# Local transformers on one core: transposes of 64 rows into two banks at a time, scores and transposes on two shared pairs of banks

## What is computed

```python
def _L0_ffn_ref(x, Wqkv, q_scale, k_scale, Wo, ln_g, ln_b, W1, b1, W2, b2):
    DIM, DEPTH, HEADS, DIM_HEAD, WINDOW, QK_SCALE = 128, 6, 16, 64, 32, 8.0
    def attn_layer(x, Wqkv, qs, ksc, Wo):
        q, k, v = split(x @ Wqkv)                    # 3 x 1024 channels, 16 heads of 64
        q = l2norm(q) * qs; k = l2norm(k) * ksc
        q = q * cos * scale + rotate_half(q) * sin * scale
        k = k * cos / scale + rotate_half(k) * sin / scale
        # a window of 32 queries sees the 32 keys of its window and the 32 before it
        sim = einsum('bhwie,bhwje->bhwij', q, k2) * QK_SCALE
        attn = softmax(where(mask, -max, sim), -1)
        return einsum('bhwij,bhwje->bhwie', attn, v2).reshape(...) @ Wo
    def ffn_layer(x, g, bln, W1, b1, W2, b2):
        xn = layernorm(x) * g + bln
        a, gate = split(xn @ W1 + b1)
        return a * gelu(gate) @ W2 + b2
    for i in range(DEPTH):
        x = attn_layer(shift_tokens(x), Wqkv[i], ...) + x
        x = ffn_layer(shift_tokens(x), ln_g[i], ...) + x
    return x
```

## Times and profile before

| what | value |
|---|---|
| runs (3) | 4911.07, 4916.79, 4919.24 us; median 4916.79 us |
| profiled execution | 4911.92 us, of which its span on the core 4909.9 us |
| first local transformer, first to last `down` (L1097) | 694.3 to 2389.1 us |
| second local transformer, first to last `down` | 2786.9 to 4480.5 us |
| one period in the steady state | 36.75 us |
| busy in that period | PE 35.10, PEld 25.04, DVE 32.91, ACT 32.21, POOL 24.49 us |
| granted TensorE clock there | 1.00 of 2.4 GHz |

### The profile page before, as it was taken

One profiled execution on the slowest core, in us unless ns is written; L12 is line 12 of the kernel. 1 busy time (PEld: TensorE's weight loads), 2 busy tenths in 40 slices (PEclk: granted clock), 3 DMA queues, 4 the chain that ended last, 5 costly groups with the idle time before them and its releaser, 6 DMA issues. The chain is left out here.

```text
span 4909.9 us, 119405 instructions
## 1 busy us (share of the span) xinstructions
PE 4169.3 (85%) x39531; PEld 2777.5 (57%) x39531; DVE 4164.4 (85%) x13469; ACT 3550.5 (72%) x10708; POOL 2949.9 (60%) x2774
## 2 busy tenths in 40 slices
PE   5888799999999999999504999999999999996675
PEld 2222266666666666666301666666666666663353
DVE  5999889989989989988497889889889889884657
ACT  4666388888888888888301888888888888884121
POOL 2777576666666666666254666666666666660323
PEclk7999899999999999999756999999999999997787
DMA  1000110101111110110001101111110100100000
GB/s 25 0 0 0 40 28 21 49 21 34 36 34 30 28 42 21 28 30 21 9 0 40 28 21 43 28 34 30 41 30 21 48 23 22 35 21 9 5 3 9
DMA packets 69277, 120.92 MB, mean 25 GB/s; under 512 B 24872, under 2 KB 46052, under 8 KB 67172
## 3 DMA queue, kind: packets, MB, share of 16 engines
q1 hardware_dynamic: 68708, 113.70, 8.9%
HBM read 35.56 MB, written 1.05 MB: 7 GB/s over the span
## 5 line engine op out<-in xcount | busy, mean ns | idle before, releaser
L1170 ACT ACTIVATE local_pr<-local_sm,local_nmax 128x96 f32<-128x96 f32 x3072 | 1115.8, 378 | 25.0 <-DVE local_nmax L1315 23.7
L926 POOL TENSOR_TENSOR local_qk<-local_qk,local_rb 128x512 f32<-128x512 f32 x768 | 973.7, 1274 | 239.5 <-DVE local_rb L1291 228.2
L937 POOL TENSOR_TENSOR local_pr<-local_pr,local_rsum 128x384 f32<-128x384 f32 x768 | 635.4, 837 | 714.1 <-DVE local_rsum L1322 714.1
L932 POOL TENSOR_TENSOR local_qk<-local_qk,local_rinv 128x512 f32<-128x512 f32 x768 | 779.8, 1041 | 261.3 <-DVE local_rinv L204 261.3
L997 PE MATMUL local_pj<-local_wqkv,local_xs 128*128 128x512 f32 x1536 | 820.0, 617 | 97.2 <-ACT local_v L1162 53.8
L1154 ACT ACTIVATE local_sq<-local_pj 128x512 f32<-128x512 f32 x768 | 448.3, 597 | 309.7 <-PE local_pj L997 243.6
L1288 DVE TENSOR_TENSOR local_qk<-local_pj,local_rope 128x512 f32<-128x512 f32 x768 | 526.2, 685 | 167.5 <-ACT local_sq L1154 139.1
L1315 DVE CUSTOM_DVE_ANT_0 local_sm<-local_sc,local_mask 128x96 f32<-128x96 f32 x3072 | 603.2, 252 | 71.0 <-PE local_sc L1019 62.3
L1170 ACT ACTIVATION_READ_ACCUMULATOR local_pr<-local_sm,local_nmax 128x1 f32 x3072 | 627.1, 204 | 0.0
L1291 DVE TENSOR_TENSOR local_rb<-local_pj,local_rope 128x512 f32<-128x512 f32 x768 | 522.3, 680 | 0.0
L1027 PEld LDWEIGHTS local_tb<-net_ident,local_pr 128*128 128x128 f32 x3072 | 362.1, 141 | 267.8 <-issue 222.1
(11 more groups left out here) (379 smaller groups left out, 8112.2 us busy)
## 6 DMA issues: line engine op xcount, KB each, us to landing
local_v<-local_v SPq DMA_DIRECT2D x288, 256.0 KB, 3.8
local_wqkv<-L_ffn_Wqkv_dram SPq DMA_DIRECT2D x12, 1536.0 KB, 8.7
local_wo<-L_ffn_Wo_dram SPq DMA_DIRECT2D x12, 512.0 KB, 5.2
local_w<-L_ffn_W_dram SPq DMA_DIRECT2D x12, 341.0 KB, 3.0
mamba_parts<-mamba_in_low SPq DMA_DIRECT2D x12, 128.0 KB, 2.3
local_w<-L_ffn_W_dram SPq DMA_DIRECT2D x12, 128.0 KB
y_dram<-store_xtok SPq DMA_DIRECT2D x4, 256.0 KB, 2.5
local_oT<-rope_dram SPq DMA_DIRECT2D x2, 256.0 KB, 3.2
```

Of the source, the lines that this page charges most:

```text
L926: nc.gpsimd.tensor_tensor(qk[:, u, :], qk[:, u, :], rb[:, u % 2, :], ALU.add).then_inc(s["summed"], 1)
L932: nc.gpsimd.tensor_tensor(heads8(qk[:, u, :]), heads8(qk[:, u, :]), r, ALU.mult).then_inc(s["scaled"], 1)
L937: nc.gpsimd.tensor_tensor(at, at, view(rsum[:, k // 2, k % 2, 0:1], [[1, 4], [0, KW]]), ALU.mult).then_inc(s["weighted"], 1)
L1170: ins = nc.scalar.activation(pr[:, (NU * c + k) % PR_RING, i, WIN:WIN + KW], sm[:, k % SM_RING, i, :], ACT.Exp, scale=-1.0, bias=nmax[:, k ...
```

## The change

All of it is in `local_transformer`.

- A transpose of 128 x 128 becomes two transposes of 64 rows: the upper 64 rows of the operand go to one bank of a pair, the lower 64 rows to the other, 128 partitions x 64 columns each. Two units are done in one call (`turn_qk`, `turn_probs`), so a call is 16 transposes that fill both banks, and a period has 4 + 4 calls where it had 8 + 8.
- `sc` is gone. `tb` is now two pairs of banks, and scores, probabilities and q/k take the pairs by turns in the order of the list `PAIRS_OF_BANKS` (12 uses in a period). A use waits until the pair's use before has been read whole: `maxima` of both units, or both copies.
- `copy_probs` and `copy_qk` still copy one bank of 512 words each, 8 + 8 in a period; a bank now holds 64 tokens of 8 blocks where it held 128 of 4. `prT` keeps its size as 2 couples x 2 halves.
- The moved rows of v are counted on two semaphores, one for even and one for odd sequences, where there was one.
- The lists `PROJECTIONS` and `iteration` of all five engines are written anew, with other lags.

```diff
@@ -685,7 +685,7 @@
-PT_RING = 4
+PT_RING = 2
@@ -694,13 +694,15 @@
-TURNS = [("probs", 3, 1), ("qk", 2, 5), ("probs", 3, 2), ("probs", 3, 3), ("qk", 2, 6), ("probs", 3, 4),
...
+PAIRS_OF_BANKS = [("qk", 3, 1), ("score", 3, 0), ("probs", 4, 1), ("qk", 3, 2), ("probs", 4, 2), ("qk", 3, 3),
+         ("probs", 4, 3), ("score", 3, 1), ("probs", 3, 0), ("score", 3, 2), ("qk", 2, 0), ("score", 3, 3)]
...
+FREED = {"score": "maxed", "probs": "probs_copied", "qk": "qk_copied"}
@@ -782,7 +784,7 @@
-        prT = m.sb("prT", [P, PT_RING, 4 * P])
+        prT = m.sb("prT", [P, PT_RING, 2, BANK])
@@ -798,11 +800,10 @@
-        sc = [m.ps(f"sc{i}", [P, BANK]) for i in range(2)]
-        tb = [m.ps(f"tb{i}", [P, BANK]) for i in range(2)]
+        tb = [[m.ps(f"tb{i}{j}", [P, BANK]) for j in range(2)] for i in range(2)]
@@ -972,12 +975,12 @@
-            def free_turn_bank(kind, seq, k):
-                last = before(TURNS, (kind, k), seq, 2)
+            def free_pair(kind, seq, k):
+                last = before(PAIRS_OF_BANKS, (kind, k), seq, 2)
                 if last:
-                    pe.wait_ge(s[last[0] + "_copied"], last[1])
-                return turn_bank(kind, k)
+                    pe.wait_ge(s[FREED[last[0]]], 2 * last[1])
+                return pair_of_banks(kind, k)
@@ -1008,7 +1011,7 @@
-                need(pe, s["maxed"], NU * c + 2 * kk)
+                sc = free_pair("score", c, kk)
@@ -1020,11 +1023,14 @@
-            def turn_probs(c, par, k):
-                bank = free_turn_bank("probs", c, k)
-                pe.wait_ge(s["weighted"], NU * c + k + 1)
-                for i in range(4):
-                    ins = nc.tensor.transpose(bank[:, i * P:(i + 1) * P], pr[:, (NU * c + k) % PR_RING, i, :], net.ident[:, :])
+            def turn_probs(c, par, kk):
+                banks = free_pair("probs", c, kk)
+                pe.wait_ge(s["weighted"], NU * c + 2 * kk + 2)
+                for h in range(2):
+                    for i in range(4):
+                        for low in range(2):
+                            rows, at = slice(low * QB, (low + 1) * QB), (4 * h + i) * QB
+                            ins = nc.tensor.transpose(banks[low][:, at:at + QB], pr[rows, (NU * c + 2 * kk + h) % PR_RING, i, :], net.ident[rows, rows])
@@ -1098,51 +1107,43 @@
             def iteration(run):
-                run(turn_probs, 3, 1)
-                run(project, 1, 5)
-                run(turn_qk, 2, 5)
...
+                run(project, 2, 2)
+                run(out_project, 5, 1)
+                run(turn_qk, 3, 1)
...
@@ -1187,15 +1189,15 @@
-                pairs, first = slice(half * 4, half * 4 + 4), t * P + which * WIN
-                nc.scalar.activation((qT, kT)[which][:, par, pairs, first:first + P], bank[:, :].rearrange("p (a t) -> p a t", a=4),
-                                     ACT.Copy).then_inc(s["qk_copied"], 1)
+                first = t * P + which * WIN + low * QB
+                nc.scalar.activation((qT, kT)[which][:, par, :, first:first + QB],
+                                     pair_of_banks("qk", j)[low][:, :].rearrange("p (a t) -> p a t", t=QB), ACT.Copy).then_inc(s["qk_copied"], 1)
```

More of the change, by code:

```diff
@@ L1143, in iteration @@
-                run(turn_qk, 1, 4)
-                run(out_project, 3, 1)
-                run(project, 0, 4)
+                run(project, 2, 2)
+                run(out_project, 5, 1)
+                run(turn_qk, 3, 1)
+                run(project, 2, 3)
+                run(centre, 5, 0)
+                run(score, 3, 0)
+                run(turn_probs, 4, 1)
+                run(variance, 5, 0)
+                run(project_v, 3, 2)
+                run(project_v, 3, 3)
+                run(weigh, 4, 0)
@@ new lines, in iteration @@
+                run(project, 2, 4)
+                run(turn_qk, 3, 2)
+                run(project, 2, 5)
+                run(turn_probs, 4, 2)
+                run(weigh, 4, 1)
+                run(project, 2, 6)
+                run(spread, 5, 0)
+                run(turn_qk, 3, 3)
+                run(project, 2, 7)
+                run(up, 5, 0)
+                run(turn_probs, 4, 3)
+                run(score, 3, 1)
+                run(weigh, 4, 2)
+                run(project_v, 2, 0)
@@ L1147, in _ @@
+                run(up, 5, 1)
+                run(project_v, 2, 1)
+                run(turn_probs, 3, 0)
+                run(weigh, 4, 3)
+                run(score, 3, 2)
+                run(up, 5, 2)
+                run(project, 1, 0)
+                run(project, 1, 1)
+                run(down, 5, 0)
+                run(turn_qk, 2, 0)
+                run(score, 3, 3)
+                run(out_project, 4, 0)
             pipeline(pe, iteration)
@@ L1216, in iteration @@
+                run(copy_probs, 3, 5)
+                run(copy_qk, 2, 6)
+                run(copy_qk, 2, 7)
+                run(square, 1, 7)
+                run(gelu, 4, 0)
+                run(gelu, 4, 1)
+                run(copy_probs, 3, 6)
+                run(copy_probs, 3, 7)
+                run(copy_o, 3, 2)
+                run(gelu, 4, 2)
                 run(copy_probs, 2, 0)
                 run(copy_v, 1, 0)
+                run(copy_probs, 2, 1)
+                run(copy_v, 1, 1)
@@ L1424, in iteration @@
                 run(recip, 3, 2)
-                run(sum_squares, 1, 3)
-                run(rotate, 1, 4)
+                run(rotate, 1, 2)
+                run(rotate, 1, 3)
+                run(maxima, 2, 0)
+                run(std, 4, 0)
+                run(std, 4, 1)
             for i in range(2):
```

275 lines of the change are left out of this document (113 added, 162 removed).

## The result

| | before | changed kernel |
|---|---|---|
| time, median of 4 runs | 4917.15 us | 4973.51 us (4970.01 to 4975.05) |
| ratio | | 1.0116, 95% interval 1.0098 to 1.0133 |
| span of the profiled execution | 4909.9 us | 4971.1 us |
| one period | 36.75 us | 37.47 us |

A forecast was written before the change was run, and what follows sets the result against it. TensorE's own work was taken to set the period, 88 times 36.75 us. Transposes -3.25 and shapes +1.9 give -1.35 us a period, 119 us in all: 4797 us, range 4690 to 4960 for 8 in 10.

The forecast's parts named there:

- The block of half transposes: In `turn_qk` and `turn_probs`, 16 half transposes take 0.47 us, or 0.6 to 0.65 to the next group's start.
- The second rival: In the turns, half transposes load like ordinary weights or don't go side by side: 5030 to 5080 us, chance 0.11.
- PE's work: On TensorE, work in a period falls from 34.7 to 33.4 us: transposes -3.25, shape changes +1.9.
- the three standstills: TensorE's waits before: 0.78 us for `copy_v`'s bank, 0.81 for the diagonal, 0.46 for `scale`; 2.0 us a period.
- ScalarE: On ScalarE, the same copies at 0.60 us and the same table loads: work stays at 32.2 us a period.
- The wait for `copy_v`: Between TensorE's `project`s, the 0.78 us wait for the bank that `copy_v` frees should go.
- VectorE and GpSimd run the same instructions in another order: nothing in work: On VectorE and GpSimd, reordering adds no work; VectorE stays at 32.9 us a period.
- 2.0 us kept: On TensorE, new waits about as large as those that go: stalls stay 2.0 us a period.
- the twelve uses of the pairs: At the shared PSUM bank pairs, tightest are `score(3,3)` with some room and `turn_qk(3,3)`, 3.8 us, nearly nothing to spare.
- the third: At the shared pairs, TensorE waits for `maxima` or a second copy: stalls 4.2 us, 4990 us in all, chance 0.09.
- The value of PE's work: TensorE's 1.35 us less work shortens each of 88 periods by as much: a gain of 119 us.
- Forecast 35.4: The period of the whole kernel: 33.4 us of TensorE work plus 2.0 us of stalls.

The follow-up runs named there:

- experiment 1: GpSimd's `add_parts`, `scale` and `norm_p` cut to 16 columns of a row, in the changed kernel (4716.42 us) and in the kernel before (4780.03 us).
- experiment 8: Changed kernel with three `scale`s moved ahead of `add_parts`, plus whole transposes: 4828.19 us; plus `tensor_reduce` shifts instead: 4807.05; those shifts and `residual2` earlier: 4804.14.
- `scale`s first: Changed kernel with GpSimd's `scale` 4 to 6 moved ahead of `add_parts(0, 0)`, nothing else: 4785.20 us.

## Why the prediction was wrong

- **The block of half transposes: right.** 0.64 us from start to start, at the top of the 0.6 to 0.65 given; halves do load and stream side by side, with a load as short as a whole transpose's (a median of 139 for 141 ns). The second rival is out. By the Trainium skill's rule on loads (TensorE: Matmul & The Clock Gate, section LDWEIGHTS) a block would be 0.86 us as an estimate; the rows of these transposes don't agree with it.
- **PE's work: the sum right, the saving not.** It is 33.6 us by experiment 1 for the 33.4 summed, shape changes included. But before had 34.4, not 34.7: the three standstills that I read fall about 0.35 us short of all its stalls. So PE saves 0.8 us of the 1.35 forecast, and the two errors hide each other in the sum.
- **ScalarE: right.** 32.34 for 32.21 us busy. The wait for `copy_v` went, as I said.
- **"VectorE and GpSimd run the same instructions in another order: nothing in work": the step that failed.** VectorE's busy time rose from 32.91 to 34.09 us, and on the chain on which PE waits the collisions rose from 3.06 to 5.20 us. The sign was in the trace of before: `maxima` and reductions there have one duration each, while L204 has a mean of 508 ns for 128 x 2 elements. I read busy times and no group's spread.
- **"2.0 us kept": wrong, as the consequence.** The stalls are 3.9 us. Without the collisions they would be 1.21 for before's 0.87; the rest is theirs. I argued from how full the engines are and looked only at the twelve uses of the pairs. As far as the runs show, all but 0.06 us of the stalls lie elsewhere, so the rival for which I had worked out this size (the third: 4.2 us, 4990 us) had the right number by another mechanism; a forecast by it would have been right by luck.
- **The value of PE's work: too high.** I took 1.35 us of work as 1.35 us of period. Whole against half transposes, in the same lists, are 0.46 and 0.47 us, and without the long GpSimd instructions the whole change is worth 0.45: a faster PE waits longer. With as many collisions as before, the gain would have been some 40 us, not 119.
- **The miss, added up.** Forecast 35.4, measured 37.47 us a period: 2.07 us. Of these 1.17 are the collisions that the new lists add (experiment 1), and 0.90 is a gain of 0.45 where I had 1.35.

Left open: what holds the period at 34.8 us where PE works 33.6 and no other engine over 32.1 (PE's stalls there are ahead of `out_project` and of `centre`, and experiment 8 only moved the first); and how the +1.18 us of the new lists would split between the lists and the pairs, since no run has one without the other. That moving three GpSimd instructions returns 2.1 us shows that the order alone can cost as much.

## What to carry to other kernels

Where VectorE and GpSimd work at once, an order is also a choice of what runs beside what: lay the lists of the two engines side by side and keep GpSimd's long instructions away from VectorE's short ones that read and write SBUF on a chain that TensorE waits for. In a trace, a small instruction with a mean far over its minimum is the sign, and its excess is part of the sum. A saving on the busiest engine is worth its full size only if that engine hardly waits.

## What was not expected of the hardware

- A VectorE instruction of 128 x 2 elements took 1.20 us beside a GpSimd `tensor_tensor`, and 0.16 alone. Reversing the order of the elements changed nothing (a mean of 664 ns for 664, a shortest of 290 for 290). Reductions of one element (415 ns) didn't wait, nor did `rotate`, which reads PSUM and SBUF: 676 and 678 ns in the changed kernel, 676 and 680 with the `scale`s first.
- GpSimd's own instructions kept their durations: `add_parts` 1272 ns in both of these kernels. Only VectorE's side showed the wait.
- Two fp32 transposes of 64 rows stream side by side: 16 in 0.64 us less the change of shape, against 0.87 for eight whole ones.
